# A gated SwiGLU with int8-style quantisation: weight scales folded on GpSimd, silu and the quantisation's products on ScalarE

## The reference, cut to what matters

```python
def _dynamic_quant(x, inv_smooth):
    xs = x.astype(jnp.float32) * inv_smooth
    scale = jnp.maximum(jnp.max(jnp.abs(xs), axis=-1, keepdims=True) / QMAX, 1e-08)
    q = jnp.clip(jnp.round(xs / scale), -QMAX, QMAX)
    return (q, scale)

def _quant_gemm(q, x_scale, w_q, w_scale):
    acc = q @ w_q.T
    return acc * x_scale * w_scale[None, :]
...
    x_flat = x.reshape(-1, H).astype(jnp.bfloat16)          # H = 512
    qg, sg = _dynamic_quant(x_flat, inv_gate)
    qu, su = _dynamic_quant(x_flat, inv_up)
    gate_out = _quant_gemm(qg, sg, w_gate, s_wgate)         # 256 columns
    up_out = _quant_gemm(qu, su, w_up, s_wup)
    inter = jax.nn.silu(gate_out) * up_out
    inter = jnp.clip(inter, -10.0, 10.0).astype(jnp.bfloat16)
    qi, si = _dynamic_quant(inter, inv_inter)
    return _quant_gemm(qi, si, w_down, s_wdown)
...
    x = x + tanh(g_xattn[1]) * _L1_xattn_ref(_layernorm(x), ctx, ctx, ...)
    x = x + tanh(g_ffn[1]) * _L1_ffn_ref(_layernorm(x), ...)
```

## Time and profile before

| what | value |
|---|---|
| median of 3 runs | 1120.84 us |
| the profiled execution's own time | 1123.95 us |
| its span, first to last instruction | 1122.1 us |
| mean granted TensorE clock | 0.962 of full speed |
| busy PE, DVE, ACT, POOL | 91%, 59%, 43%, 33% of the span |

### The profile page before, as it was taken

One profiled execution on the slowest core, in us unless ns is written; L12 is line 12 of the kernel. 1 busy time (PEld: TensorE's weight loads), 2 busy tenths in 40 slices (PEclk: granted clock), 3 DMA queues, 4 the chain that ended last, 5 costly groups with the idle time before them and its releaser, 6 DMA issues. The chain is left out here.

```text
span 1122.1 us, 18616 instructions
## 1 busy us (share of the span) xinstructions
PE 1019.9 (91%) x6780; PEld 880.7 (78%) x6780; DVE 658.2 (59%) x1128; ACT 484.6 (43%) x943; POOL 371.4 (33%) x252
## 2 busy tenths in 40 slices
PE   5899999999999999999999999998998579999964
PEld 4888989889798898988989889896777357777543
DVE  5475566457456546745745664673475546667396
ACT  4365346336435534733643563461231125555311
POOL 4207305503620830560363074041891300000054
PEclk9999999999999999999999999998998689999986
DMA  6002001100200200110020021000621183121000
GB/s 206 1 1 95 1 1 56 37 0 5 88 0 0 93 0 0 56 37 0 0 93 0 0 61 51 0 1 1 197 76 38 38 205 63 30 56 30 1 1 37
DMA packets 29617, 46.49 MB, mean 41 GB/s; under 512 B 3216, under 2 KB 12048, under 8 KB 29584
## 3 DMA queue, kind: packets, MB, share of 16 engines
q1 hardware_dynamic: 29008, 46.03, 13.8%
q10 hardware_dynamic: 576, 0.00, 0.0%
HBM read 41.83 MB, written 4.19 MB: 41 GB/s over the span
## 5 line engine op out<-in xcount | busy, mean ns | idle before, releaser
L430 DVE TENSOR_TENSOR ptL<-tbank,ptH 128x512 fp32r<-128x512 f32 x192 | 132.2, 688 | 84.4 <-ACT ptH L290 84.3
L290 ACT ACTIVATE ptH<-tbank 128x512 fp32r<-128x512 f32 x192 | 115.8, 603 | 109.4 <-PE tbank L539 109.1
L205 POOL TENSOR_TENSOR oTL<-o_norm,oTH 128x512 fp32r<-128x512 f32 x32 | 41.3, 1291 | 350.4 <-ACT oTH L310 350.4
L539 PE MATMUL tbank<-ident,probs 128*128 128x128 f32 x864 | 132.2, 276 | 16.6 <-DVE ptL L430 12.2
L443 DVE TENSOR_REDUCE negmax<-score 128x1 f32<-128x768 f32 x128 | 119.5, 948 | 19.7 <-PE score L74 19.7
L401 DVE TENSOR_REDUCE sumsq<-probs 128x2 f32<-128x256 f32 (+1 forms) x80 | 42.1, 526 | 136.9 <-ACT probs L285 71.8
L316 ACT ACTIVATE probs<-score,negmax 128x768 f32<-128x768 f32 x128 | 115.6, 903 | 15.5 <-DVE negmax L443 15.5
L72 PE MATMUL obank<-ptH,vH 128*128 128x256 f32 x384 | 122.2, 318 | 0.0
L539 PEld LDWEIGHTS tbank<-ident,probs 128*128 128x128 f32 x864 | 98.3, 140 | 26.5 <-DVE ptL L430 15.1
L74 PE MATMUL score<-wkvH,kvT_lo 128*128 128x256 f32 x384 | 108.7, 283 | 0.0
L73 PE MATMUL score<-wkvL,kvT_hi 128*128 128x256 f32 x384 | 108.7, 283 | 0.0
(11 more groups left out here) (252 smaller groups left out, 2469.3 us busy)
## 6 DMA issues: line engine op xcount, KB each, us to landing
wqo_stage<-in_wq SPq DMA_DIRECT2D x9, 1024.0 KB, 5.7
wqo_stage<-in_wo SPq DMA_DIRECT2D x8, 1024.0 KB, 5.2
wkv_stage<-in_wkv SPq DMA_DIRECT2D x9, 512.0 KB, 6.5
a_qS<-q_scratch SPq DMA_DIRECT2D x32, 128.0 KB, 3.8
ctx_stage<-in_ctxT SPq DMA_DIRECT2D x2, 1024.0 KB, 13.6
kS<-k_scratch SPq DMA_DIRECT2D x32, 64.0 KB, 2.2
q_scratch<-part SPq DMA_DIRECT2D x8, 256.0 KB, 4.1
wqo_stage<-in_down_w SPq DMA_DIRECT2D x3, 512.0 KB, 4.6
```

What stands on the lines that cost most here:

```text
L290: act.activation(out, tbank[c % 2][:], ACT.Copy, scale=scale).then_inc(t_hi, 1)
L430: i = dve.tensor_tensor(out, tbank[c % 2][:], f32(hi), ALU.subtract)
L539: i = pe.transpose(tbank[c % 2][:, n * P:(n + 1) * P], block_in, S.ident[:])
```

## The change

Five things are edited.

1. The column scales of the gate and up weights, and of the down weights with the gate's tanh, are multiplied into the weights. `fold` does it on POOL, ahead of all of POOL's part of the last stage, and makes the fp32r part and the remainder of each piece too: six pieces, three instructions each. `split_hi` and `split_lo` are gone from ACT and DVE.
2. ACT makes silu from PSUM in one instruction with the row's scale; DVE multiplies the up half with its scale and with silu in one instruction. The exponential, the addition of one, the reciprocal and POOL's two products are gone.
3. In both quantisations the product with the inverse (plus the rounding constant) is ACT's, from SBUF and back in place, and DVE keeps maximum, scale, inverse and clip.
4. DVE adds the down product times its scale to x at once; POOL's last addition is gone.
5. The order written for `stagger` is another on every engine, the second quantisation comes one step sooner, and PE's waits are adapted.

```diff
-    def split_hi(self, act, n):
-    def split_lo(self, dve, n):
...
+    def fold(self, pool):
+        zero = self.S.zero[:].to_broadcast([P, 2 * INT1])
+        pool.wait_ge(self.vec_in, 6 * 16)
+        pool.tensor_tensor(self.s_down[:], self.s_down[:], self.S.tanh_g[:, 3:4].to_broadcast([P, HID]),
+                           ALU.mult).then_inc(self.gated, 1)
+        pool.wait_ge(self.w_in, 3 * 16)
+        pool.wait_ge(self.gated, 1)
+        for n, (stage, scales, hi, lo) in enumerate(self.w_pieces()):
+            pool.tensor_tensor(stage, stage, scales[:], ALU.mult).then_inc(self.w_folded, 1)
+            pool.wait_ge(self.w_folded, n + 1)
+            pool.tensor_tensor(hi, stage, zero, ALU.add).then_inc(self.w_hi, 1)
+            pool.wait_ge(self.w_hi, n + 1)
+            pool.tensor_tensor(lo, stage, f32(hi), ALU.subtract).then_inc(self.w_lo, 1)
...
-        self.stagger(((statistics, 0), (layernorm, 1), (quantise_x, 2), (clip, 4), (gate_up, 3),
-                      (quantise_inter, 4), (output, 5), (sigmoid, 3)))
+        def times_up(t):
+            dve.wait_ge(self.pe_gu, 2 * t + 2)
+            dve.wait_ge(self.silu_done, t + 1)
+            dve.scalar_tensor_tensor(self.silu[:, t, :], free.obank[t % 2][:, INT1:2 * INT1], self.scale[:, t, 1:2],
+                                     self.silu[:, t, :], ALU.mult, ALU.mult).then_inc(self.up_done, 1)
+            dve.wait_ge(self.up_done, t + 1)
+            dve.tensor_scalar(self.inter[:, t, :], self.silu[:, t, :], 10.0, -10.0, ALU.min, ALU.max).then_inc(self.inter_done, 1)
...
+            dve.scalar_tensor_tensor(S.X[:, t, :], free.halves[t], self.scale2[:, t:t + 1], S.X[:, t, :],
+                                     ALU.mult, ALU.add).then_inc(self.out_ready, 1)
+        self.stagger(((statistics, 0), (clip_inter, 4), (layernorm, 1), (largest_x, 2), (times_up, 3),
+                      (output, 5), (clip_x, 2), (largest_inter, 3)))
...
-        self.stagger(((rsqrt, 0), (weights, 1), (weights2, 4), (output, 5), (swiglu, 3)))
+        self.stagger(((rsqrt, 0), (weights, 1), (weights2, 3)))
...
+        def scale_x(t):
+            act.wait_ge(self.q_step, 3 * t + 3)
+            for i in range(2):
+                act.activation(free.q[:, t, i, :], free.q[:, t, i, :], ACT.Copy, bias=ROUND,
+                               scale=self.inv[:, t, i:i + 1]).then_inc(self.scaled, 1)
+        def silu(t):
+            act.wait_ge(self.pe_gu, 2 * t + 2)
+            act.activation(self.silu[:, t, :], free.obank[t % 2][:, 0:INT1], ACT.Silu,
+                           scale=self.scale[:, t, 0:1]).then_inc(self.silu_done, 1)
+        def scale_inter(t):
+            act.wait_ge(self.q2_step, 3 * t + 3)
+            act.activation(self.q2[:, t, :], self.q2[:, t, :], ACT.Copy, bias=ROUND,
+                           scale=self.inv2[:, t:t + 1]).then_inc(self.scaled2, 1)
...
-        self.stagger(((exp, 3), (copy_qT, 2), (copy_q2T, 4)))
+        self.stagger(((silu, 3), (scale_x, 2), (copy_q2T, 4), (copy_qT, 2), (scale_inter, 3)))
...
-            pe.wait_ge(self.qT_done, 2 * min(t + 3, RT))
+            pe.wait_ge(self.qT_done, 2 * min(t + 2, RT))
...
-        self.stagger(((transpose_q, 2), (gate_up, 2), (transpose_q2, 4), (down, 4)))
+        self.stagger(((transpose_q2, 4), (transpose_q, 2), (down, 4), (gate_up, 2)))
...
+            ffn.fold(pool)
             ffn.gpsimd(pool)
```

More of the change, by code:

```diff
@@ L1005, in w_pieces @@
         S = self.S
-        return ([(S.wqo_stage[:, k, :], self.wguH[:, k, :], self.wguL[:, k, :]) for k in range(KT)]
-                + [(self.wdn_stage[:, k, :], self.wdnH[:, k, :], self.wdnL[:, k, :]) for k in range(INT1 // P)])
+        return ([(S.wqo_stage[:, k, :], self.s_gu, self.wguH[:, k, :], self.wguL[:, k, :]) for k in range(KT)]
+                + [(self.wdn_stage[:, k, :], self.s_down, self.wdnH[:, k, :], self.wdnL[:, k, :]) for k in range(INT1 // P)])
     def loads(self, sp):
@@ L1045, in vector @@
         S, free = self.S, self.free
-        q, gate, up = free.q, free.gate, free.up
+        q = free.q
         def statistics(t):
@@ L1059, in layernorm, with largest @@
                               ALU.subtract, ALU.mult).then_inc(self.xb_done, 1)
-        def quantise(rows, scale, inv, step, done, base):
-            n = rows.shape[1]
+        def largest(rows, scale, inv, step, base):
             dve.tensor_reduce(scale, rows, AX.X, ALU.max, apply_absolute_value=True).then_inc(step, 1)
@@ L1068, in quantise @@
             dve.reciprocal(inv, scale).then_inc(step, 1)
[L1069 to L1075, removed]
-            dve.wait_ge(self.weighted, 2 * t + 2)
-            quantise(q[:, t, :, :], self.scale[:, t, :], self.inv[:, t, :], self.q_step, self.q_done, 5 * t)
@@ L1079, in gate_up @@
-        def gate_up(t):
-            dve.wait_ge(self.pe_gu, 2 * t + 2)
[L1081 to L1095, removed]
@@ L1269, in attn1 @@
     free = Shared()
-    free.q, free.qT, free.tmp = expo[:, 0:RT, :].rearrange("p t (i n) -> p t i n", i=2), qS, o_rows
+    free.q, free.qT = expo[:, 0:RT, :].rearrange("p t (i n) -> p t i n", i=2), qS
     free.score, free.obank, free.halves = score, obank, halves
-    free.gate, free.up = (oT[:, 2 * i:2 * i + 2, :].rearrange("p k n -> p (k n)").rearrange("p (t n) -> p t n", t=RT)
-                          for i in range(2))
     free.wguH, free.wguL = (m[:].rearrange("p k n -> p (k n)")[:, 0:KT * 2 * INT1]
@@ L1341, in turn @@
                     act.activation(expo[:, v % NE_, :], scoreT[v % 2][:], ACT.Exp).then_inc(s_exp, 1)
-                    if last and v < len(ffn.w_pieces()):
-                        ffn.split_hi(act, v)
             turns(act, turn)
@@ L1386, in turn @@
                         window(2 * i + 2, 0)
-                    if last and v < len(ffn.w_pieces()):
-                        ffn.split_lo(dve, v)
             def finish_quad(i, r, w):
```

58 lines of the change are left out of this document (21 added, 37 removed).

## The result

The changed kernel takes 1108.25 us in the median of 4 runs (1108.12 to 1110.65); the kernel before, beside it, 1120.07. The ratio is 0.9896, with a 95% interval of 0.987 to 0.9923. Predicted were 1110.5 us, between 1106 and 1117, and faster by over 0.5% with a chance of 0.84.

The account below looks back on a forecast made before the run. The last stage was taken to wait on a chain with DVE as its heaviest link; -2.3 + 0.4 - 2.05 + 0.2 - 6.5 = -10.25 us gave 1110.5 us, own range 1108 to 1113, 8 in 10 within 1106 to 1117.

Parts of the forecast that it names:

- Part 1 and 2: Attention loop: splits gone from ACT and DVE give -2.3 us; the fold on POOL costs DVE +0.4 us.
- The fold's price: Loop: only DVE's copy of a_vcol waits, on average half a POOL instruction of 1.26 us; +0.4 us taken.
- Part 3: Last stage, tile 0: silu reads the bank itself and starts at 1080.2 in place of 1082.25, -2.05 us.
- at half rate: Tile 0: PE's first transposes begin at about 1075.5 as before, at half rate, 1.94 us against 1.10.
- The table load: Tile 0, ACT: the 1.28 us load ahead of silu is over by 1079.4 and hidden.
- Part 4: Last stage, silu of tile 0 to silu of tile 3: rounds 7.9, 8.2, 7.3, sum 23.4 against 23.2, +0.2 us.
- The closed round: Each tile passes silu, ACT's pair, DVE's clip, PE's transposes and matmuls before the next silu; 6.2 us at full clock.
- the inverse that was to come 0.9 late: Tile 2's round: its inverse late behind tile 3's normalisation, the maximum and tile 0's clip on DVE; round 8.2 us.
- One sign of being wrong: Last stage, PE: transposes of tiles 2 and 3 taking 1.9 would show the steps wrong.
- Part 5: From silu of tile 3 to DVE's last addition: 7.7 us in place of 14.2, -6.5 us.
- (1): Rival: TensorE at half clock through tiles 1 to 3, +6.2 us, gain 4.1, 1116.7 us; chance 0.17.
- (3): Rival: TensorE at full clock from tile 0's matmuls to the end, 1107.5 us; chance 0.14.

Follow-up runs that it names:

- e5: Changed kernel with 70 more two-input products of 512 columns on POOL behind the fold, in the attention loop; one run, 1106.39 us.
- e3: Changed kernel with silu by parts again: gate and exponential on ACT, addition and reciprocal on DVE, product on POOL; 1.0033 of the kernel before.
- e2: Changed kernel with the quantisation's products back on DVE, right behind the inverse; 0.9892 of the kernel before.
- e4: Changed kernel with matmuls of no use on PE in the pauses ahead of the transposes; 0.9863 of the kernel before.
- e6: Changed kernel with its new functions in the order of the kernel before; 0.988 of the kernel before.

## Why the prediction was right

**Part 1 and 2, the loop:** -2.3 + 0.4 predicted, -2.46 measured, -2.0 to -2.5 over all kernels, all against the one trace of before. The group with four splits alone gave -2.32. The fold's price was put at half a POOL instruction and is nothing measurable, even with 70 more (e5): the wait of the copy is real, but PE is busy for 24.90 of the fold's 25 us, and DVE's idle time can take it.

**Part 3, tile 0:** -2.05 predicted, -3.42 measured. Its step "at half rate" failed: PE ran the first transposes at full clock after 3.05 us of idle. From their start to the end of the sixteen matmuls are 3.46 us for 4.61 before, which is -1.15; they started 0.20 earlier; and the time from the end of the matmuls to silu fell by 2.07, where the prediction has 2.05. e5, with the same stage and half clock there, has -1.31. The table load was hidden as said, by 0.45 us.

**Part 4, the rounds:** +0.2 predicted, +1.67 measured (24.90 for 23.23). The closed round is right: the chain of waits runs through it, e3 lengthened it by what was put into it, and e2 shows that DVE's relief gave nothing. The size was off in the clock. I had half clock in tile 1 alone, for its transposes and half of its matmuls: 7.9, measured 8.50, with all sixteen at half clock. Tile 3 had its transposes at half clock too: 7.3 and 8.18. Tile 2's 8.2 against 8.22 is luck, for two errors cancel: its down product and matmuls took 4.36 us for the 3.26 assumed, ten of the sixteen at half clock, and the inverse that was to come 0.9 late was ready 0.8 us before silu ended. One sign of being wrong, transposes of tiles 2 and 3 at 1.9, came for tile 3. What the first tile won, the rounds lost; in e5 it is the other way round, and the stages differ by 0.34 us. That the sum came out although parts 3 and 4 missed by 1.4 and 1.5 us, in opposite directions, is luck as well.

**Part 5, the end:** -6.5 predicted, -6.51 measured, 7.7 against 7.68. It is the largest term, a chain of single instructions whose durations stood in the trace. It is right to 0.02 us in part because small misses cancel: the transposes took 0.47 us until ACT began, where 0.78 were priced, and silu, the product and the handovers took more. It also holds only for the lower clock in the last down product, 2.17 us as before; at full clock throughout, in e4, the end is 6.81.

**The sum:** -10.25 predicted, -10.7 in the two traces, -11.8 in the runs' medians, with an interval from -8.6 to -14.6. The 1.1 us of the runs' gain that show in neither stretch are small against that interval; their cause is open.

**The rivals.** TensorE at half clock throughout (1) did not come, nor at full clock throughout (3): the clock went between its two levels within the rounds. e4 shows what full clock throughout is worth against the changed kernel as it ran: 5.3 us. The Trainium skill's "SBUF — State Buffer", section "Who interferes with whom", holds here: copies waited, 128 maxima did not. What it says of an instruction with one SBUF input is limited to those outside the two-port modes, which the prediction leaves out. The extra drain that the Trainium skill's "ScalarE: Activation LUTs", section "What ACT_TABLE_LOAD costs", adds to the load does not show: in e6 the load starts 0.01 us behind the products, takes 1.28, and silu starts at once.

## What to carry to other kernels

Where engines run their lists in order, price a change by the closed round from one tile to the next and by the last tile's lonely chain, not by the busy time that an engine sheds: 16.8 us off DVE gave 8.3, and 6.5 of these came from the last tile alone. Then test the order apart from the functions: the same functions in another order gave 9.8 us more than the change as it was made, 4.4 of them at an equal clock. Look for an instruction of an early tile that stands behind the work of a later one.

## What the runs showed of the hardware

The length of an idle time did not tell the clock by itself: after 3.05 us PE came back at full clock in the changed kernel and, after 3.06, at half clock in e6; within the changed kernel, after 2.35 full and after 2.56 half; and in e5, with the same stage, tile 3's transposes came at full clock after 2.57. An estimate of a clock-bound term needs both levels as its bounds. The time ahead of the change varied by 6.5 us between the profiled executions of the changed kernel and its variants, by 8.8 with before, over the same instructions; so a span is no measure of a change of this size.
